# Soft mixture of experts, first part, on one core: row-paired weight products, normalisation in two operations per tile, two-scalar copies

## The reference

```python
xn = _layernorm(x, ln_gamma, ln_beta)
x_unit = _l2norm(xn, axis=-1)
mu_unit = _l2norm(mu, axis=0)
logits = jnp.einsum('bnd,des->bnes', x_unit * scale, mu_unit)
dispatch = jax.nn.softmax(logits, axis=1)
combine = jax.nn.softmax(logits.reshape(B, N, E * S), axis=-1).reshape(B, N, E, S)
slot_in = jnp.einsum('bnd,bnes->besd', xn, dispatch)
h = jax.nn.gelu(jnp.einsum('besd,edh->besh', slot_in, w1) + b1[None, :, None, :], approximate=False)
slot_out = jnp.einsum('besh,ehd->besd', h, w2) + b2[None, :, None, :]
out = jnp.einsum('besd,bnes->bnd', slot_out, combine)
```

```python
q, k, v = (jnp.einsum('ntc,hdc->nhtd', x, w) for w in (w_q, w_k, w_v))
a = jax.nn.softmax(masked(jnp.einsum('nhtd,nhsd->nhts', q, k) / 8), axis=3)
y = jnp.einsum('nhts,nhsd->nthd', a, v).reshape(n, t, -1) @ w_o
```

## Time and profile before

| | |
|---|---|
| median of 3 runs | 1026.29 us (1025.15 to 1029.08) |
| profiled execution | 1024.24 us, its span 1022.5 us |
| busy share PE, DVE, ACT, POOL | 81%, 73%, 55%, 20% of the span |
| mean granted TensorE clock | 0.912 |
| `expert_scores` | from 560.6 to 630.2 us of the span |

### The profile page before, as it was taken

The page is one execution under the profiler, slowest core; times in us unless marked ns, Lnnn a source line. Parts: engine busy times, 40 slices in busy tenths (PEclk is TensorE's granted clock), DMA queues, the critical chain, the costliest instruction groups (busy, mean ns, idle before and its releaser), DMA issues. The chain is left out here.

```text
span 1022.5 us, 26783 instructions
## 1 busy us (share of the span) xinstructions
PE 823.2 (81%) x9567; PEld 490.9 (48%) x9567; DVE 746.9 (73%) x2473; ACT 562.1 (55%) x1398; POOL 204.5 (20%) x217
## 2 busy tenths in 40 slices
PE   5899999995975788696663397896986999999686
PEld 2577777774322233242131275563664555555343
DVE  5688888884389999999996795456463667767757
ACT  3788898886675658575240476453343333333244
POOL 1467766663000000000000011002210000000136
PEclk9999999998897788898797598997897999999889
DMA  7111111100000000000000903100570000000001
GB/s 241 33 44 43 40 37 41 41 6 2 1 0 0 1 1 0 1 1 0 1 0 8 166 2 117 52 5 19 205 274 1 1 1 0 0 0 1 1 11 31
DMA packets 23157, 36.54 MB, mean 36 GB/s; under 512 B 5668, under 2 KB 19748, under 8 KB 20644
## 3 DMA queue, kind: packets, MB, share of 16 engines
q1 hardware_dynamic: 23080, 35.53, 11.6%
HBM read 34.48 MB, written 1.05 MB: 35 GB/s over the span
## 5 line engine op out<-in xcount | busy, mean ns | idle before, releaser
L381 ACT ACTIVATE xa_prob<-xa_s,xa_nmax 128x257 f32<-128x257 f32 x256 | 128.1, 503 | 21.6 <-DVE xa_nmax L466 19.8
L568 POOL TENSOR_TENSOR xa_prob<-xa_prob,xa_rinv 128x1028 f32<-128x1028 f32 x64 | 121.5, 1900 | 75.8 <-DVE xa_rinv L473 74.6
L466 DVE CUSTOM_DVE_ANT_0 xa_s<-xa_s_ps,xa_nbias 128x257 f32<-128x257 f32 x256 | 93.2, 420 | 12.3 <-ACT xa_prob L381 6.4
L1492 POOL TENSOR_TENSOR mo_disp_t<-mo_disp_t,mo_rst 128x256 f32<-128x256 f32 x16 | 9.9, 616 | 377.0 <-DVE mo_rst L1472 377.0
L2117 PEld LDWEIGHTS ca_z_ps<-ca_xn_t,ca_m_t 128*128 128x128 f32 x512 | 62.0, 198 | 30.5 <-issue 26.0
L2200 ACT COPY ca_z<-ca_z_ps 128x512 f32<-128x512 f32 x64 | 37.5, 585 | 69.0 <-PE ca_z_ps L2117 69.0
L242 PE MATMUL xa_t_ps<-identity,xa_prob 128*128 128x128 f32 x512 | 69.4, 279 | 3.7 <-ACT xa_p_t L390 2.1
L2117 PE MATMUL ca_z_ps<-ca_xn_t,ca_m_t 128*128 128x128 f32 x512 | 67.9, 288 | 4.1 <-ACT ca_xn_t L2194 3.9
L456 DVE COPY xa_kvs<-xa_kv_ps 128x512 f32<-128x512 f32 x64 | 44.1, 689 | 34.5 <-PE xa_kv_ps L216 34.5
L242 PEld LDWEIGHTS xa_t_ps<-identity,xa_prob 128*128 128x128 f32 x512 | 54.8, 141 | 25.3 <-issue 25.3
L390 ACT COPY xa_p_t<-xa_t_ps 128x1024 f32<-128x1024 f32 x64 | 63.4, 990 | 2.7 <-PE xa_t_ps L242 2.7
(11 more groups left out here) (327 smaller groups left out, 1929.1 us busy)
## 6 DMA issues: line engine op xcount, KB each, us to landing
xa_ctx_t<-in_ctx_t SPq DMA_DIRECT2D x64, 128.5 KB, 2.1
room<-in_ctx_t SPq DMA_DIRECT2D x8, 1028.0 KB, 6.6
room<-in_ctx_n SPq DMA_DIRECT2D x8, 1024.0 KB, 4.8
ss_wx<-in_ss_wx SPq DMA_DIRECT2D x1, 2048.0 KB, 7.8
xres<-in_x SPq DMA_DIRECT2D x4, 256.0 KB, 5.5
out_x<-xres SPq DMA_DIRECT2D x4, 256.0 KB, 2.3
ma_mask_u<-in_mask SPq DMA_DIRECT2D x4, 128.5 KB
room<-in_ca_wk SPq DMA_DIRECT2D x1, 512.0 KB, 4.9
```

The lines of the kernel that those rows point to most:

```text
L381: nc.scalar.activation(prob[:, r, g, :], s_sb[:, b, g, :], ACT.Exp, bias=nmax[:, r, g:g + 1], scale=-1.0, accum_out=rsum[:, r, g:g + 1]).t ...
L466: nc.vector.tensor_tensor_reduce(out=s_sb[:, b, g, :], in0=s_ps[:, g, 0:S], in1=nbias[:, g, :], scale=1.0, scalar=3e38, op0=ALU.add, op1=A ...
L568: nc.gpsimd.tensor_tensor(prob[:, r, :, :], prob[:, r, :, :], bc(rinv[:, r, :].rearrange("p (g o) -> p g o", o=1), (P, G, S)), ALU.mult).t ...
```

## The change

- Normalisation: per tile two scalar_tensor_tensor operations, `centred` = (x - mean) * gamma and `normed` = that * rstd + beta. `centred` needs no rstd; nine of them are placed among the statistics operations, and `normed(t)` and `centred(t+9)` alternate after that. `nmr` isn't made. ScalarE's squares wait for one tile each, and use two junk buffers.
- `unit(t+3)` goes from VectorE to ScalarE (between `exps` and `out`), but for the first three tiles.
- `maxima` does the batch maxima first, then the row maximum. `rs_own` is dropped; the two copies to `comb_own` take rs and the parity column as two scalars.
- Joins: w_q, w_k, w_v, w_o lie on 128 partitions, two heads above each other (8 pairs). Even heads' products run on rows 0 to 63 and odd heads' on rows 64 to 127, into the upper halves of two PSUM banks: even heads to the bank that `l_ps` has for n % 2, odd ones to a third bank. The row maximum of tile t + 2 waits until the join of tile t is copied out.
- Copies of the joins: even n on ScalarE as before, odd n on VectorE, at the end of its iteration.

```diff
+        def two_banks(n):
+            return lj_ps[:, n % 2:3:2 - n % 2, SLOTS:2 * SLOTS].rearrange("p s (i c) -> p s i c", i=2)
...
-        l_ps, lt_ps = k.ps("mo_l_ps", [P, 2, 512]), k.ps("mo_lt_ps", [P, 2, 512])
-        j_ps = k.ps("mo_j_ps", [P, 512])
+        lj_ps, lt_ps = k.ps("mo_lj_ps", [P, 3, 512]), k.ps("mo_lt_ps", [P, 2, 512])
+        l_ps = lj_ps[:, 0:2, :]
...
                 for h in range(HG):
-                    last = nc.tensor.matmul(j_ps[:, h * D:h * D + D], left[:, HG * q + h, :], right[:, HG * q + h, :],
-                                            start=True, stop=True)
+                    rows, head = slice(64 * (h % 2), 64 * (h % 2) + 64), (HG * q + h) // 2
+                    last = nc.tensor.matmul(lj_ps[:, 2 if h % 2 else n % 2, SLOTS + h // 2 * D:SLOTS + h // 2 * D + D],
+                                            left[rows, head, :], right[rows, head, :], start=True, stop=True)
...
-            for q in range(4):
-                act.wait_ge(xn_ready, q + 1)
-                for t in range(4 * q, 4 * q + 4):
-                    if t:
-                        act.wait_ge(sums_ready, t)
-                    nc.scalar.activation(junk[:, :], x1[:, t, :], ACT.Square, accum_out=nrm[:, t:t + 1]).then_inc(sums_ready, 1)
+            for t in range(T):
+                act.wait_ge(xn_ready, t + 1)
+                if t >= 2:
+                    act.wait_ge(sums_ready, t - 1)
+                nc.scalar.activation(junk[:, t % 2, :], x1[:, t, :], ACT.Square, accum_out=nrm[:, t:t + 1]).then_inc(sums_ready, 1)
...
+            def unit(t, j):
+                if t >= 2:
+                    act.wait_ge(xut_mm, t - 1)
+                nc.scalar.activation(xu[:, j, :], x1[:, t, :], ACT.Copy, scale=sums[:, t:t + 1]).then_inc(xu_ready, 1)
...
+            def centred(t):
+                nc.vector.scalar_tensor_tensor(x1[:, t, :], xres[:, t, :], mv[:, t, 0:1], gamma[:, :], ALU.subtract, ALU.mult).then_inc(xg_ready, 1)
+
+            def normed(t):
+                dve.wait_ge(xg_ready, t + 1)
+                nc.vector.scalar_tensor_tensor(x1[:, t, :], x1[:, t, :], rstd[:, t:t + 1], beta[:, :], ALU.mult, ALU.add).then_inc(xn_ready, 1)
...
-            for q in range(4):
-                for t in range(4 * q, 4 * q + 4):
-                    last = nc.vector.tensor_scalar(x1[:, t, :], xres[:, t, :], rstd[:, t:t + 1], nmr[:, t:t + 1], ALU.mult, ALU.add)
-                last.then_inc(x1_ready, 1)
...
+            centred(8)
+            dve.wait_ge(rstd2_ready, 2)
+            for t in range(T):
+                normed(t)
+                if t + 9 < T:
+                    centred(t + 9)
...
+            def joined_values(n):
+                dve.wait_ge(join_mm, n + 1)
+                nc.vector.tensor_copy(w_vo[:, :, n // 2, :].rearrange("p (i s) c -> p s i c", s=2), two_banks(n)).then_inc(join_ready, 1)
...
+                if FIRST <= t - 2 < FIRST + JOINS:
+                    dve.wait_ge(join_ready, t - 1 - FIRST)
+                if t >= 2:
+                    dve.wait_ge(exp_ready, t - 1)
+                nc.vector.tensor_reduce(mx[:, j:j + 1], l_ps[:, j, 0:SLOTS], AX.X, ALU.max, negate=True).then_inc(mx_ready, 1)
...
-                nc.vector.tensor_scalar(rs_own[:, j, :], parity[:, :], rs[:, j:j + 1], None, ALU.mult).then_inc(own_ready, 1)
-                dve.wait_ge(own_ready, t + 1)
...
-                                                   comb[:, j, :].rearrange("p (g e s) -> p g e s", g=4, e=4), rs_own[:, j, b:b + 1], None, ALU.mult)
+                                                   comb[:, j, :].rearrange("p (g e s) -> p g e s", g=4, e=4), rs[:, j:j + 1], parity[:, b:b + 1], ALU.mult, ALU.mult)
...
-    w_q, w_k, w_v, w_o = (room[0:64, n * 16 * D:(n + 1) * 16 * D].rearrange("p (h c) -> p h c", h=16) for n in range(4))
+    w_q, w_k, w_v, w_o = (room[:, n * 8 * D:(n + 1) * 8 * D].rearrange("p (h c) -> p h c", h=8) for n in range(4))
```

More of the change, by code:

```diff
@@ L1238, in expert_scores @@
         eps = k.sb("mo_eps", [P, 1])
-        junk = k.sb("mo_junk", [P, D])
+        junk = k.sb("mo_junk", [P, 2, D])
+        def two_banks(n):
+            return lj_ps[:, n % 2:3:2 - n % 2, SLOTS:2 * SLOTS].rearrange("p s (i c) -> p s i c", i=2)
         xu, xu_t = k.sb("mo_xu", [P, 2, D]), k.sb("mo_xu_t", [P, 2, P])
-        mx, sm, rs, rs_own = k.sb("mo_mx", [P, 2]), k.sb("mo_sm", [P, 2]), k.sb("mo_rs", [P, 2]), k.sb("mo_rs_own", [P, 2, 2])
+        mx, sm, rs = k.sb("mo_mx", [P, 2]), k.sb("mo_sm", [P, 2]), k.sb("mo_rs", [P, 2])
         comb = k.sb("mo_comb", [P, 2, SLOTS])
@@ L1347, in _, with joined_scores @@
             nc.scalar.preload_act_table(ACT.Exp)
-            def joined_part(n):
+            def joined_scores(n):
                 q = n // 2
                 act.wait_ge(join_mm, n + 1)
[L1352 to L1356, removed]
+                nc.scalar.activation(m_t[:, HG * q:HG * q + HG, :].rearrange("p (i s) c -> p s i c", s=2), two_banks(n), ACT.Identity,
+                                     scale=64.0 ** -0.5).then_inc(join_ready, 1)
             def xut(t, j):
@@ L1386, in _ @@
                     exps(t + 1, 1 - t % 2)
+                if t + 3 < T:
+                    unit(t + 3, 1 - t % 2)
                 out(t, t % 2)
-                if FIRST <= t < FIRST + JOINS:
-                    joined_part(t - FIRST)
+                if FIRST <= t < FIRST + JOINS and t % 2 == 0:
+                    joined_scores(t - FIRST)
         @block.vector
@@ L1394, in _ @@
             nc.vector.memset(eps[:, :], EPS).then_inc(const_ready, 1)
-            norm.vector(dve)
+            nc.vector.memset(norm.eps[:, :], EPS).then_inc(norm.eps_set, 1)
+            def centred(t):
[3 more added lines that the diff above has]
+                nc.vector.scalar_tensor_tensor(x1[:, t, :], x1[:, t, :], rstd[:, t:t + 1], beta[:, :], ALU.mult, ALU.add).then_inc(xn_ready, 1)
@@ L1397, in _ @@
+            dve.wait_ge(w_ld, W_LD)
+            centred(0)
+            centred(1)
+            dve.wait_ge(norm.root_ready, 1)
+            nc.vector.reciprocal(rstd[:, :], norm.root[:, :]).then_inc(norm.ready, 1)
+            centred(2)
+            dve.wait_ge(norm.ready, 1)
             nc.vector.tensor_tensor(var2[:, :], mv[:, :, 1], rstd[:, :], ALU.mult).then_inc(var2_ready, 1)
+            centred(3)
             dve.wait_ge(var2_ready, 1)
             nc.vector.tensor_tensor(var2[:, :], var2[:, :], rstd[:, :], ALU.mult).then_inc(var2_ready, 1)
+            centred(4)
@@ L1400, in _ @@
+            centred(5)
+            centred(6)
             dve.wait_ge(root_ready, 1)
             nc.vector.reciprocal(sums[:, :], sums[:, :]).then_inc(rstd2_ready, 1)
+            centred(7)
             dve.wait_ge(rstd2_ready, 1)
             nc.vector.tensor_tensor(rstd[:, :], rstd[:, :], sums[:, :], ALU.mult).then_inc(rstd2_ready, 1)
[L1404 to L1407 removed]
@@ L1472, in scales @@
                 nc.vector.reciprocal(rst[:, j, :], smt[:, j, :]).then_inc(rst_ready, 1)
+            dve.wait_ge(unit_ready, 1)
             unit(0, 0)
             unit(1, 1)
+            unit(2, 0)
             maxima(0, 0)
-            unit(2, 0)
             scales(0, 0)
@@ L1481, in _ @@
                     maxima(t + 1, 1 - t % 2)
-                if t + 3 < T:
-                    unit(t + 3, 1 - t % 2)
                 if t + 1 < T:
                     scales(t + 1, 1 - t % 2)
+                if FIRST <= t < FIRST + JOINS and t % 2 == 1:
+                    joined_values(t - FIRST)
         @block.gpsimd
```

23 lines of the change are left out of this document (9 added, 14 removed).

## The result

The changed kernel takes 1022.51 us (median of 20 runs, 1013.5 to 1028.55); the kernel before, in 20 runs on the same chips, 1026.36. The recorded ratio is 0.9955, with a 95% interval of 0.9933 to 0.9977 (the two medians alone give 0.9963, inside it): 1021.7 us on the scale of the median before, 1019.4 to 1023.9 by the interval, where 1021.8 was predicted. The profiled execution of the changed kernel took 1017.3 us (span 1015.5), 6.9 less than that of before. Only part of this is the change, as the windows show: the stage's first half, its loop, and then the four later stages in turn.

A forecast was written before the change was run, and what follows sets the result against it. Bounds: a serial chain in the first half; in the loop VectorE without joins, TensorE with them. 1024.24 - 5.4 + 0.9 = 1019.7 us, on the medians' scale 1026.29 - 4.5 = 1021.8; range 1018.6 to 1025.4.

The forecast's parts named there:

- First half: Normalisation, up to the first `unit`: the new operation order gains 5.4 us; 7.3 or 2.5 with other operation prices.
- Tile without a join: Loop tile without a join: 2.76 us, 0.08 less than now, with VectorE waiting for the exponentials before `rs`.
- The rival in which those waits close (2): Loop: every wait left in the tile closes, second column free, no join waits; -6.5 us, 1019.8; chance 0.22.
- The rival in which the column costs more (3): Loop: row pairs run serially (1023.6 us) or the second column costs 126 ns (1023.8); both 1025.6; chance 0.18.
- Join: Joins on TensorE: two row groups run side by side, 0.70 us, and 0.64 to the next instruction instead of 1.09.
- Join pair: Two loop tiles with joins: 6.12 us of VectorE work plus 0.1 waiting before its copy.
- the sentence that VectorE's own copy delays the maximum past ScalarE's copy: Steady join tiles: the row maximum comes after ScalarE's copies anyway; only the first costs, 0.4 us.
- the prediction's sentence that TensorE is no longer the bound: Tiles with joins: TensorE's share falls to 2.6 us, so it no longer bounds them.
- Loop: Whole loop: 0.9 us longer, from joins +0.8, tiles without joins -0.2, head +0.3; bounds -1.2 and +2.8.
- the head: Loop's start: `maxima` needs the second logits product first, which comes last on TensorE at half clock; +0.3 us.
- the loop's lower bound: Best case for the loop: second scalar column free (15 x 0.13) and no waits at the joins' start; -1.2 us.
- rival 4: Loop: pauses hold TensorE at half clock, a join tile needs 5.2 us; +26 us, 1048; chance 0.08.

The follow-up runs named there:

- the new order: Changed kernel with its loop operations reordered on VectorE, ScalarE and TensorE, all join copies on ScalarE: 1013.77 us, ratio 0.9864 to the kernel before.

## Why the prediction was right, step by step

**First half: 5.4 predicted, 5.7 measured.** The SCALAR_TENSOR_TENSOR, priced at 351 ns and 0.26 apart from rows of other shapes, took 332 and 341 ns on average, 0.26 apart. The first `normed` came 2.87 us after the memset (563.07), where 3.21 had been put down (560.59 to 563.8), and VectorE's chain ended the half, as said. The whole 0.3 lies in that start: the first `centred` comes 0.10 after the memset instead of 0.18, and the statistics' small operations cost 0.09 each in the row of `centred` (560.30 to 563.07 less nine times 0.26), where I had put down 0.13.

**Tile without a join: 2.76 predicted, 2.75 to 2.76 measured,** with the wait before `rs` and 0.13 us for the second scalar columns. The rival in which those waits close (2) did not happen, and the row maximum first shows that the wait was the price of the maxima's new order, not of the hardware: 2.51 without it. The rival in which the column costs more (3) fell with the 0.74 for two copies.

**Join: 0.70 and 0.64 predicted, 0.71 and 0.64 measured.** Two groups of 64 rows do run side by side.

**Join pair: 6.22 predicted, 6.25 measured, but with another wait.** I had VectorE wait 0.1 for the join before its copy, and the row maximum not at all after the first join. The rows show the reverse: no wait before the copy, 0.13 before the row maximum. The step that failed is the sentence that VectorE's own copy delays the maximum past ScalarE's copy. ScalarE comes to that copy only after the exponentials, `unit` (which the change gave it) and both copies of `out`.

Whether a join is waited for can be read from its copy: where it is, in the new order, the copy starts 0.05 us after the join's end. In the changed kernel's steady pairs VectorE's starts 0.11 after it (600.85 + 0.72 = 601.57, copy at 601.67) and ScalarE's 0.34. So neither waits, and the prediction's sentence that TensorE is no longer the bound holds, though with only 0.06 to spare in every second tile. What holds the pair is a ring on VectorE and ScalarE: from the row maximum at 596.30 through ScalarE's exponentials, `unit`, `out` and copy of the join (to 599.16) to the row maximum at 599.19, 2.89; then through the exponential of the rows, VectorE's `rs`, scaled copies, sums, `rst` and own copy of the join to the next row maximum, 3.36.

Three experiments bear this out. With `unit` back on VectorE the first link shrinks to 2.75, and then the wait that I had predicted does appear (copy 0.21 behind `rst`, 0.05 after the join); the pair is 6.24 by this second limit, 0.01 from the first. That 6.22 came so near the 6.25 is in part luck: two limits lie side by side. With all copies on ScalarE both copies of a pair start 0.05 after their join's end, the join is in the ring, and a pair is 3.59 (`rst` at 596.86 through GpSimd, `turn`, logits, join and copy to the row maximum at 600.45) + 2.36 = 5.95. With one row group the later join eats the 0.06 and delays VectorE's copy: 6.68. (Any closed ring adds up to the length of the pair; it is the missing waits along it that make it the one that holds.) With the row maximum first ScalarE's link is the longer one: row maximum, both exponentials, `unit`, `out`, copy, next row maximum, 3.28 us, because the exponential of the slots waits 0.22 for a later subtraction; where VectorE copies the join out, its own work in that tile is nearly as long, 3.27 with 0.09 of waiting. The joins end 0.5 before their copies there. That wait was not tried by itself.

**Loop: +0.9 predicted, +0.85 measured.** Its pieces, counted from `rst` to `rst`: the eight intervals with joins 24.75 to 25.29 us, +0.54 (+0.8 predicted); the seven without, -0.22 (-0.2 with the two last); the head, to the first `rst`, +0.26 (+0.3 predicted); the tail +0.25 (nothing predicted). For the joins 4 x 6.22 + 0.4 = 25.28 was right; what was wrong is the kernel before, where I took 8 x 3.06 = 24.48 and the first of the eight takes 3.24. The tail's 0.25 is the clock. The two errors of 0.25 cancelled: the loop's sum is right by luck to that extent. So is the total to 0.1 us: its interval is 2.3 us to each side, and the later stages moved by more than that.

Two side sums of the prediction don't add up by their own terms, without consequence: the loop's lower bound (0.9 - 1.95 - 0.4) is -1.5 rather than -1.2, and rival 2 with the join waits of 0.8 also gone is -7.3 rather than -6.5.

**The clock (rival 4).** The granted clock was 0.92 on average over the loop, and 1.00 in the stretch with the joins, though TensorE had gaps there:

```profile
572.30:579.00 6.70, 5.54 (x19) 4.28 (x19) 3.74 (x13) 1.67 (x6) 0.38 (x1) 0.54 1.20 140
579.00:590.00 11.00, 8.32 (x53) 6.51 (x52) 9.51 (x33) 8.30 (x28) 2.44 (x5) 1.00 0.01 1
590.00:615.00 25.00, 21.93 (x168) 17.14 (x169) 21.52 (x68) 19.05 (x60) 5.17 (x9) 1.00 0.00 1
```

The last stretch is at the full 2.4 GHz with TensorE busy 21.93 of 25.00 us, where it was 24.50 of 24.50 before. The rise came 6.2 us into the loop; in the kernel before 7.3 (8.1 in its second profile), not the 6.8 that the prediction read from the edge of a window. In the tiles with joins rival 4 did not happen. At the loop's end it did in small: over the 10.90 us before the fall at 50.6 TensorE was busy 7.64, and the last products then ran at 1.2 GHz, 0.25 us in the tail; with one row group the fall came at 47.9, after 10.50 us with 8.51 busy, and cost 0.5. In the first profile of the kernel before it came at 51.7, behind the last products.

**Where the joins' gain went.** Eight joins are 3.6 us shorter. Against the same order with one row group 1.7 of it arrive in the tiles with joins; VectorE's copies take back 1.4 there; the changed order of the maxima takes 0.24 in each tile without a join. The Trainium skill, page TensorEngine Tiling (Array Packing), section PSUM Bottleneck, has it that tiled matmuls may run into the emptying of PSUM; the traces agree in part: the copies were worth 1.4 us by their engine alone, but once the order was changed, with the same 128x512 copies, 3.4 of the 3.6 us arrived. The limit was the order, more than the copies.

## What to carry to other kernels

Before moving work off a full engine, look at what it fills there: `unit` lay in a wait, so moving it bought nothing until the order around it changed. Follow a shared buffer's release round the whole ring, over as many tiles as it has buffers, and ask at each link whether it waits: a copy that starts 0.05 behind its product waits for it, one that starts 0.34 behind does not, and there a faster product gives nothing. When engines show gaps of 10 to 15% each in one loop, try the order of the streams before the price of the operations: here it gave 9.2 us on three engines together, no single edit of the loop more than 1.6.

## What was not expected of the hardware

- `expert_layers` takes 68.7 to 74.4 us with the same instructions, and TensorE stops inside one group of matmuls, waiting for nothing that the profile shows. From the kernel before:

```profile
646.88 0.63 PE L1549 MATMUL me_in_ps<-me_slot_in,me_w 128*32 128x64 f32 x27 [0.19 <-ACT me_slot_in L1594]
...
648.66 0.31 PE L1549 MATMUL me_in_ps<-me_slot_in,me_w 128*32 128x64 f32 x5 [1.14 <-issue]
```

  The two profiles of the changed kernel and the two of the new order have no such stop over 0.15 us (68.7 to 69.4), the two of before and the eight of other variants have three to five (73.3 to 74.4). In the kernel before five of them sum to 3.96 us, about the whole difference of 3.87. Each stop over 0.3 us, in all ten of these profiles, begins 0.8 to 2.2 us after a 16 KB packet of the instruction queue (q8) starts; but the stage has 16 such packets in every profile, in those without stops too. The cause is open. It also blurs the totals: with the row maximum first the stage is 5.8 us shorter than before the change, and the timed kernel 3.1 (1.1 to 5.0).
- The joins' weights, the same 512 KB each, land faster as 128 rows of 4 KB than as 64 of 8 KB. From issue to landing the four took 4.9, 6.9, 8.8 and 11.2 us before and 3.5, 4.4, 5.4 and 6.4 after, in the order of their issue; the kernels with one row group, which go back to 64 rows, took 5.0 to 11.1 again. It was hidden in both.
